# Row coefficients laid out by kind, sequence and token before GpSimd reads them across x by features

## The chip, the cores and the metric

One core of a Trainium2 chip runs the whole program. The metric is the device time in microseconds of one execution, from its start to its end.

## The reference, cut to what matters

The input x has 4 sequences of 4096 tokens of 512 features. A causal linear attention block and a linear layer with quantised operands follow each other, each between two layer norms and with a residual:

```python
x = x + layernorm(attn(layernorm(x)))          # linear attention, 16 heads of 32, elu(.)+1 feature map
x = x + layernorm(ffn(layernorm(x)))           # ffn: 512x512, both operands quantised in blocks of 32
# attn: q, k, v = x @ W.T + b; running sums over tokens of k v^T and of k;
#       out = (q . kv_cum) / max(q . k_cum, 1e-6);  then @ Wo.T + bo
```

The part that the change touches is the first layer norm. It has one scale and one shift for each token: `x * rstd(token) + shift(token)`.

## The kernel before, in words

The work is cut into 32 tiles. A tile is 128 tokens of each of the 4 sequences, so 512 rows of x. A loop of turns is written out by hand: turn i does the matmuls of q, k, v, scores, attention and output of tile i, the linear layer of tile i-1, and the norm of x for tile i+1. Each engine has its own list of instructions in a fixed order, and semaphores join the lists. TensorE (PE) does 240 matmuls of 128x512 in a turn and many small ones.

The norm of x is applied to x **by features**: the 128 partitions are features, and along the free axis lie 4 groups of features times 128 tokens. In that layout a token's coefficients vary along the free axis and are the same in each partition, so they have to be copied to all partitions. This goes over DRAM, in these steps:

- VectorE (DVE) takes the mean and variance of the 4 sequences of the tile, with tokens as partitions. GpSimd (POOL) makes from them `coef`, 128 partitions (tokens) x 2 kinds (scale, shift) x 4 sequences (`rstd`, L1388 and L1391).
- SyncE (SP) stores `coef` in `coef_dram` (`store_coef`, L331), waits until it has landed, and loads all its 1024 numbers into each of the 128 partitions of `x_coef` (`spread_coef`, L337).
- SP loads x by features into `exp_t`, a buffer with two places (`load_xt`, L327).
- GpSimd multiplies `exp_t` by the scales (L1412) and adds the shifts (L1414), for each of the 4 sequences (`x_scale`). ScalarE (ACT) and DVE then split the result into `xT_hi` and `xT_lo` (L676, L960), the operands of the next tile's matmuls.

In a turn GpSimd does `x_scale` of sequences 0 and 1 between the outputs of tile i-1 (`output`, L1442) and `x_scale` of 2 and 3 after the first residual (`residual`, L1419).

SP has one queue in a fixed order. Around the two steps it holds: store `coef`, spread it, store the output of sequence 1 of the tile before (L354), load a residual tile (L320), load two `exp_t` (L327), store `rinv`, the inverses of the attention's denominators, in DRAM (`store_rden`, L343), and spread them over `kc` (`spread_rden`, L349). What comes back is used by DVE to scale the attention of sequence 0 (`normalise`, L1024). From there two ways lead to PE: ACT casts it to `oT_hi` (L735), DVE makes `oT_lo` (L1036), and PE multiplies both with Wo; behind `oT_lo` on DVE stand the masks of the scores (L1029), for which PE's attention of sequence 1 waits (L550).

Of the kernel before, what the change touches and what calls it, by code (L numbers as in the profile page):

```python
# [5 lines left out]
F32 = mybir.dt.float32  # L6
# [6 lines left out]
P = 128  # L13
NSEQ, LEN, D = 4, 4096, 512
HEADS, DH = 16, 32
G = D // P
HPG = P // DH
TILES = LEN // P
ROWS = NSEQ * P
# [35 lines left out]
def count(tile, n, per=4):  # L55

    return tile * per + n + 1


def build(nc, x, xt, wq, wk, wv, wo, wf, bq, bk, bv, bo, bf, consts, out):  # L60
    ctx = ExitStack()
    with ctx:
        def sb(name, shape, dt=F32):
            return ctx.enter_context(nc.sbuf_tensor(name, shape, dt))
# [4 lines left out]
        def sem(name):  # L69
            return ctx.enter_context(nc.semaphore(name))  # L70
# [21 lines left out]
        x_in = sb("x_in", [P, NSEQ, D])  # L92


        x_coef = sb("x_coef", [P, P, 2, NSEQ])
        xT_hi = sb("xT_hi", [P, G, ROWS], F32R)
        xT_lo = sb("xT_lo", [P, G, ROWS], F32R)
        exp_t = sb("exp_t", [P, 2, ROWS])
# [36 lines left out]
        coef = sb("coef", [P, 2, NSEQ])  # L135
# [72 lines left out]
        coef_stored = sem("coef_stored")  # L208
# [52 lines left out]
        def by_group(flat):  # L261
            return flat.rearrange("p (g t) -> p g t", g=G)
# [25 lines left out]
        def kcq(ops, g):  # L288
            return ops.tensor_tensor(tokens(kc, g), tokens(kc, g), by_seq(QT[:, g, :]), ALU.mult)

        coef_dram = nc.dram_tensor("coef_dram", (P, 2, NSEQ), F32).ap()

        def x_cols(t, b):
            return t[:, :, b * P:(b + 1) * P]
# [9 lines left out]
        def _(sp):  # L304
# [23 lines left out]

            def store_coef(tile):
                sp.wait_ge(rstd_set["x"], count(tile, NSEQ - 1))  # L330
                sp.dma_start(coef_dram[:], coef[:]).then_inc(coef_stored, 16)  # L331

            def spread_coef(tile):
                sp.wait_ge(coef_stored, 16 * tile)
                if tile > 1:
                    sp.wait_ge(x_shifted, count(tile - 2, NSEQ - 1))
                sp.dma_start(x_coef[:].rearrange("p t k b -> p (t k b)"),  # L337
                             coef_dram.rearrange("t k b -> (t k b)").unsqueeze(0).to_broadcast([P, 2 * ROWS])
                             ).then_inc(coef_loaded, 16)

            def store_rden(tile):
# [14 lines left out]
            def turn(i, prev, cur, nxt):  # L356
# [9 lines left out]
                if nxt:  # L366
                    store_coef(i + 1)
                    spread_coef(i + 1)
# [1016 lines left out]
        def _(pool):  # L1385
# [16 lines left out]
            def turn(i, prev, cur, nxt):  # L1402
                def x_scale(tile, b):

                    def by_token(k):
                        return x_coef[:, :, k, b].unsqueeze(1).to_broadcast([P, G, P])

                    rows = by_group(exp_t[:, b % 2, :])
                    if b == 0:
                        pool.wait_ge(coef_loaded, 16 * tile)  # L1410
                    pool.wait_ge(xt_loaded[b], 16 * tile)
                    nc.gpsimd.tensor_tensor(rows, rows, by_token(0), ALU.mult).then_inc(x_scaled, 1)  # L1412
                    pool.wait_ge(x_scaled, count(tile - 1, b))
                    nc.gpsimd.tensor_tensor(rows, rows, by_token(1), ALU.add).then_inc(x_shifted, 1)  # L1414
# [179 lines left out]
```

## Time and profile before

| what | value |
|---|---|
| median of 3 runs | 2392.15 us (2386.2 to 2392.42) |
| the profiled execution, own time | 2392.45 us |
| its span in the profile | 2390.7 us |
| mean granted TensorE clock | 0.995 |
| PE busy | 2328.4 us (97%) |
| DVE busy | 1981.4 us (83%) |
| GpSimd busy | 1474.0 us (62%) |
| ACT busy | 1083.8 us (45%) |

The span is the stretch between the first and the last record of the execution; its own time is 1.75 us longer. The busy time of PE is modelled from its starts, so that a busy PE is not PE at its peak. An engine's idle time counts only where the engine that sets the end waits for it.

### The profile page before, as it was taken

To read this page: it belongs to the slowest core of one execution; us is meant where nothing else is said; L and a number is where in the kernel's file an instruction comes from. 1 tells how busy PE (TensorE), PEld (TensorE's weight loads), DVE (VectorE), ACT (ScalarE), POOL (GpSimd) and SP (SyncE) were. 2 spreads that over 40 slices of the span, in tenths; PEclk is the share of its full clock that TensorE was granted. 3 is DMA by queue.
4 is the path that set the end of the run, shared out by engine and by line. 5 is a ranking of instruction groups with operands and counts; after the bars stand their busy time and mean duration, and the time that the engine had idled before them with its cause. 6 is when DMAs were issued, how large, how long until landed. Compare 5 with 4: busy or idle time off the path is not lost.

```text
span 2390.7 us, 63829 instructions
## 1 busy us (share of the span) xinstructions
PE 2328.4 (97%) x26146; PEld 1902.4 (80%) x26146; DVE 1981.4 (83%) x3987; ACT 1083.8 (45%) x1840; POOL 1474.0 (62%) x1731
## 2 busy tenths in 40 slices
PE   7999999999999999999999999999999999999997
PEld 5878788888788788887888887888878888778885
DVE  7888788888788888888888887888888888878886
ACT  5444444444444444444444443444444444444442
POOL 4566666666566666666665665656666656656554
PEclk9999999999999999999999999999999999999999
DMA  5123222232222222222322222322123222222211
GB/s 170 60 91 100 73 83 68 75 99 87 80 71 71 91 100 73 82 67 77 99 78 90 71 69 91 99 73 82 63 82 100 73 91 73 71 91 95 77 46 36
DMA packets 108227, 195.55 MB, mean 82 GB/s; under 512 B 15136, under 2 KB 21664, under 8 KB 107424
## 3 DMA queue, kind: packets, MB, share of 16 engines
q1 hardware_dynamic: 107936, 191.47, 24.1%
q8 instruction: 206, 3.38, 0.6%
q14 instruction: 85, 0.70, 0.1%
HBM read 155.65 MB, written 35.78 MB: 80 GB/s over the span
## 4 chain that ended last, share of the span: by engine, by line
PE 77%; DMA 8%; ACT 4%; DVE 4%; issue 3%; POOL 2%; SPq 2%; POOLq 0%; DVEq 0%; ACTq 0%
PE work L428 11%; PE work L430 11%; PE work L429 11%; PE score L428 10%; PE score L429 10%; PE score L430 10%; PE work L550 4%; PE work L447 4%; DMA rden_dram<-rinv 4%; PE score L513 4%; DMA kc<-rden_dram 4%; PE state_bank L563 1%; POOL f_buf L1442 1%; ACT f_buf L680 1%; POOL rs_f L1388 1%
## 5 line engine op out<-in xcount | busy, mean ns | idle before, releaser
L1029 DVE TENSOR_TENSOR A<-score,causal 128x512 f32<-128x512 f32 x512 | 329.6, 682 | 21.3 <-PE score L513 21.1
L1412 POOL TENSOR_TENSOR exp_t<-exp_t,x_coef 128x512 f32<-128x512 f32 x124 | 198.3, 1599 | 141.4 <-DMA exp_t<-in_xt 141.4
L735 ACT CAST oT_hi<-kc 128x512 fp32r<-128x512 f32 x128 | 79.8, 624 | 365.0 <-DVE kc L1024 365.0
L1419 POOL TENSOR_TENSOR x_res<-x_res,o_buf 128x512 f32<-128x512 f32 x128 | 175.6, 1372 | 105.6 <-ACT o_buf L680 105.6
L428 PE MATMUL work<-wo_hi,oT_hi 128*128 128x512 f32 x512 | 204.6, 400 | 16.4 <-ACT Kn L730 13.6
L428 PE MATMUL work<-wv_hi,xT_hi 128*128 128x512 f32 x512 | 214.0, 418 | 0.7 <-issue 0.7
L1414 POOL TENSOR_TENSOR exp_t<-exp_t,x_coef 128x512 f32<-128x512 f32 x124 | 205.7, 1659 | 9.7
L428 PE MATMUL score<-xT_hi,wq_hi 128*128 128x512 f32 x512 | 206.8, 404 | 2.1 <-DVE KT L969 2.1
L428 PE MATMUL score<-xT_hi,wk_hi 128*128 128x512 f32 x512 | 205.9, 402 | 0.7 <-DVE xT_lo L960 0.7
L429 PE MATMUL work<-wv_lo,xT_hi 128*128 128x512 f32 x512 | 201.1, 393 | 0.8 <-issue 0.8
L430 PE MATMUL work<-wv_hi,xT_lo 128*128 128x512 f32 x512 | 201.8, 394 | 0.0
L429 PE MATMUL score<-xT_lo,wq_hi 128*128 128x512 f32 x512 | 200.8, 392 | 0.0
L430 PE MATMUL work<-wo_hi,oT_lo 128*128 128x512 f32 x512 | 200.4, 391 | 0.0
L429 PE MATMUL work<-wo_lo,oT_hi 128*128 128x512 f32 x512 | 200.3, 391 | 0.0
L430 PE MATMUL score<-xT_hi,wq_lo 128*128 128x512 f32 x512 | 200.3, 391 | 0.0
L429 PE MATMUL score<-xT_lo,wk_hi 128*128 128x512 f32 x512 | 199.8, 390 | 0.0
L430 PE MATMUL score<-xT_hi,wk_lo 128*128 128x512 f32 x512 | 199.6, 390 | 0.0
L1428 POOL TENSOR_TENSOR xd<-q,xs 128x512 f32<-128x512 fp8e4 x128 | 134.2, 1048 | 88.9 <-DVE q L1071 83.2
L1442 POOL TENSOR_TENSOR f_buf<-f_buf,x_res 128x512 f32<-128x512 f32 x96 | 136.2, 1418 | 85.6 <-ACT f_buf L680 85.6
L1388 POOL TENSOR_TENSOR rs_f<-ve_f,minus_half 128x1 f32<-128x1 f32 x128 | 81.8, 639 | 162.8 <-DVE ve_f L950 162.8
L680 ACT ACTIVATE o_buf<-x_res,shift_r,rs_r 128x512 f32<-128x512 f32 x128 | 104.5, 817 | 138.7 <-POOL shift_r L1391 138.7
L699 ACT ACTIVATE exp_t<-exp_t 128x512 f32<-128x512 f32 x256 | 162.5, 635 | 8.1
(134 smaller groups left out, 6394.9 us busy)
## 6 DMA issues: line engine op xcount, KB each, us to landing
x_in<-in_x SPq DMA_DIRECT2D x128, 256.0 KB, 4.5
kc<-rden_dram SPq DMA_DIRECT2D x128, 256.0 KB
x_res<-in_x SPq DMA_DIRECT2D x128, 256.0 KB, 2.8
exp_t<-in_xt SPq DMA_DIRECT2D x124, 256.0 KB, 3.0
out<-f_buf SPq DMA_DIRECT2D x96, 256.0 KB, 2.0
x_coef<-coef_dram SPq DMA_DIRECT2D x31, 512.0 KB, 3.6
out<-xd SPq DMA_DIRECT2D x32, 256.0 KB, 2.1
rden_dram<-rinv SPq DMA_DIRECT2D x32, 64.0 KB, 3.4
```

The costliest lines, as they stand in the source:

```text
L428: nc.tensor.matmul(dst, st_hi(c), mv_hi(c), start=(c == 0), stop=False)
L429: nc.tensor.matmul(dst, st_hi(c), mv_lo(c), start=False, stop=False)
L430: last = nc.tensor.matmul(dst, st_lo(c), mv_hi(c), start=False, stop=(c == G - 1))
L680: return nc.scalar.activation(dst, src, ACT.Identity, bias=shift[n][:, b:b + 1], scale=rs[n][:, b:b + 1])
L699: nc.scalar.activation(exp_t[:, g % 2, :], exp_t[:, g % 2, :], ACT.Exp, scale=-1.0).then_inc(exp_done, 1)
L1029: nc.vector.tensor_tensor(A[:, j, :, :], score_bank[j][:], causal[:].unsqueeze(1).to_broadcast([P, G, P]), ALU.mult).then_inc(a_set, 1)
L1388: nc.gpsimd.tensor_tensor(rs[n][:, b:b + 1], ve[n][:, b:b + 1], minus_half[:], ALU.pow).then_inc(rs_set[n], 1)
L1412: nc.gpsimd.tensor_tensor(rows, rows, by_token(0), ALU.mult).then_inc(x_scaled, 1)
L1414: nc.gpsimd.tensor_tensor(rows, rows, by_token(1), ALU.add).then_inc(x_shifted, 1)
L1419: nc.gpsimd.tensor_tensor(x_res[:, b, :], x_res[:, b, :], o_buf[:, b % 2, :], ALU.add).then_inc(r_set, 1)
L1428: nc.gpsimd.tensor_tensor(xd[:].rearrange("p (n k) -> p n k", k=BLOCK), q8[:, b, :].rearrange("p (n k) -> p n k", k=BLOCK), xs[:, b, :].un ...
L1442: nc.gpsimd.tensor_tensor(f_out[b], f_out[b], x_res[:, b, :], ALU.add).then_inc(out_set, 1)
```

## The change

The coefficients get another order in DRAM and in SBUF. Before, the 8 numbers of a token (2 kinds x 4 sequences) lay beside each other; now the 128 tokens of one kind and one sequence do. The store of `coef` writes 1024 single numbers, 8 from each partition, each 512 bytes from the next. The spread copies the same 4 KB to each partition as before. GpSimd's second operand in L1412 and L1414 had a step of 8 numbers (32 bytes) from token to token, and now has a step of 1.

```diff
-        x_coef = sb("x_coef", [P, P, 2, NSEQ])
+        x_coef = sb("x_coef", [P, 2, NSEQ, P])
...
-        coef_dram = nc.dram_tensor("coef_dram", (P, 2, NSEQ), F32).ap()
+        coef_dram = nc.dram_tensor("coef_dram", (2, NSEQ, P), F32).ap()
...
             def store_coef(tile):
                 sp.wait_ge(rstd_set["x"], count(tile, NSEQ - 1))
-                sp.dma_start(coef_dram[:], coef[:]).then_inc(coef_stored, 16)
+                sp.dma_start(coef_dram.rearrange("k b t -> t k b"), coef[:],
+                             allow_slow_non_contiguous=True).then_inc(coef_stored, 16)
...
-                sp.dma_start(x_coef[:].rearrange("p t k b -> p (t k b)"),
-                             coef_dram.rearrange("t k b -> (t k b)").unsqueeze(0).to_broadcast([P, 2 * ROWS])
+                sp.dma_start(x_coef[:].rearrange("p k b t -> p (k b t)"),
+                             coef_dram.rearrange("k b t -> (k b t)").unsqueeze(0).to_broadcast([P, 2 * ROWS])
...
                     def by_token(k):
-                        return x_coef[:, :, k, b].unsqueeze(1).to_broadcast([P, G, P])
+                        return x_coef[:, k, b, :].unsqueeze(1).to_broadcast([P, G, P])
```

No engine's list of instructions changes its order. The one instruction with another form in the list is the store on SP, which was 128x8 and is 128x8x1.

## Rows read from the trace of the kernel before

**Rows 1.** The page, part 1: busy us, share of the span, instructions.

```profile
PE 2328.4 (97%) x26146; PEld 1902.4 (80%) x26146; DVE 1981.4 (83%) x3987; ACT 1083.8 (45%) x1840; POOL 1474.0 (62%) x1731
```

**Rows 2.** Windows, 12 to 24 us after each coef store: length, PE busy; clock, DMA share, GB/s.

```profile
1008.95:1020.95 12.00, 12.00 (x228) 1.00 0.38 131
1080.87:1092.87 12.00, 10.09 (x193) 1.00 0.42 132
...
sum 372.00, PE 354.54; mean PE 11.44
...
sum 108.00, PE 102.97; mean PE 11.44
...
sum 108.00, PE 96.51; mean PE 10.72
```

**Rows 3.** The chain that ended last, in two turns: start us, us, what.

```profile
563.38 3.37 DMA rden_dram<-rinv
...
570.49 0.70 DVE kc L1024
...
571.87 2.15 DVE oT_lo L1036
...
577.73 1.08 PE work L550 x32
...
1075.92 4.84 DMA rden_dram<-rinv
```

**Rows 4.** DVE busy in L1036 alone, summed over nine stretches of 8.70 us.

```profile
sum 78.30, DVE 17.74; mean DVE 1.97
```

**Rows 5.** Timeline of GpSimd in the turn from 556.33 us.

```profile
565.89 1.65 POOL L1412 TENSOR_TENSOR exp_t<-exp_t,x_coef 128x512 f32<-128x512 f32 x1 [4.36 <-DMA exp_t<-in_xt]
...
570.14 1.56 POOL L1412 TENSOR_TENSOR exp_t<-exp_t,x_coef 128x512 f32<-128x512 f32 x1
571.78 1.69 POOL L1414 TENSOR_TENSOR exp_t<-exp_t,x_coef 128x512 f32<-128x512 f32 x1
```

**Rows 6.** Timeline of DVE and of GpSimd in the turn from 996.95 us.

```profile
1012.27 0.69 DVE L1036 TENSOR_TENSOR oT_lo<-kc,oT_hi 128x512 fp32r<-128x512 f32 x1 [0.69 <-ACT oT_hi L735]
...
1012.29 2.20 POOL L1414 TENSOR_TENSOR exp_t<-exp_t,x_coef 128x512 f32<-128x512 f32 x1
```

**Rows 7.** GpSimd's operations by tile: duration ns min/median/max, first and last start.

```profile
L1412 POOL TENSOR_TENSOR exp_t<-exp_t,x_coef x124: 1517/1611/1699, 53.9 to 2272.5; 128x512 f32<-128x512 f32 x124
L1414 POOL TENSOR_TENSOR exp_t<-exp_t,x_coef x124: 1518/1610/2229, 55.5 to 2274.2; 128x512 f32<-128x512 f32 x124
...
L1419 POOL TENSOR_TENSOR x_res<-x_res,o_buf x128: 1275/1298/1620, 70.5 to 2367.3; 128x512 f32<-128x512 f32 x128
...
L1442 POOL TENSOR_TENSOR f_buf<-f_buf,x_res x96: 1267/1290/1673, 110.2 to 2383.0; 128x512 f32<-128x512 f32 x96
```

**Rows 8.** Timeline of SP in the turn from 1216.18 us: start, us of issuing.

```profile
1216.18 0.33 SPq L331 DMA_DIRECT2D coef_dram<-coef  x1
1217.59 0.33 SPq L337 DMA_DIRECT2D x_coef<-coef_dram  x1
1221.40 0.34 SPq L354 DMA_DIRECT2D out<-f_buf  x1
...
1223.29 0.43 SPq L343 DMA_DIRECT2D rden_dram<-rinv  x1
```

**Rows 9.** Windows of the DMA engines: stretch, length, clock, share busy of 16, GB/s.

```profile
1216.18:1217.00 0.82, 1.00 0.00 0
1217.00:1217.20 0.20, 1.00 0.39 21
1217.20:1218.92 1.72, 1.00 0.02 5
1218.92:1220.66 1.74, 1.00 0.72 290
1220.66:1222.24 1.58, 1.00 0.07 23
...
1223.08:1225.48 2.40, 1.00 0.87 299
...
6.95:8.70 1.75, 1.00 1.11 328
```

**Rows 10.** SP's issues of the four weight loads at the start, min/median/max ns.

```profile
L398 SPq DMA_DIRECT2D V<-in_wk x4: 620/632/662, 3.2 to 5.3; - x4
```

## The prediction

> **What bounds the kernel now.** The page's part on busy time comes first. PE is busy in 97% of the span and GpSimd in 62% [rows 1], so 2390.7 less 2328.4, some 62 us, is all the idle time that PE has, with the start and the end of the program in it. A faster GpSimd is worth something only where PE waits, now, for what GpSimd holds up.
>
> So I looked for PE's idle time by its place in the turn. The 31 stores of the coefficients mark the turns. In the stretch from 12 to 24 us after each store PE is busy for 354.54 of 372 us, so it is idle for 17.5 us [rows 2]. I read the chain of waits and the timeline of this stretch in each turn, and the turns fall in three kinds. The second and the third sum in rows 2 are those of nine turns each:
>
> - In nine turns `oT_lo` of sequence 0 (L1036) takes 1.54 us or more, 1.97 us on average, where it takes 0.69 us elsewhere [rows 4, 6]. PE is idle for 108 less 102.97, 5.0 us, in these.
> - In nine others the store of `rinv` lands late, as the one that takes 4.84 us where another takes 3.37 [rows 3]. PE is idle for 11.5 us in these, 1.9 us in the one shown [rows 2].
> - In the other thirteen it is idle for 17.5 - 5.0 - 11.5 = 0.9 us in all; one of them has none [rows 2].
>
> The first kind is where GpSimd comes in. In the turn from 556.33 us the chain goes from the store of `rinv` over DVE's `normalise` to `oT_lo`, 2.15 us long, and on to the masks and PE's L550 [rows 3]. GpSimd began the addition of the shifts of sequence 1 at 571.78, 0.09 us before `oT_lo` at 571.87, and ended it at 573.47; `oT_lo` ended at 574.02, a little over 0.5 us after that [rows 3, 5]. In the turn from 996.95 us DVE was first by 0.02 us: `oT_lo` took its 0.69 and the addition took 2.20 us, where its median is 1.61 [rows 6, 7]. Of these two operations, whichever comes second does not run until the first is done. The Trainium skill says so too ("SBUF — State Buffer", on the shared port pair: an exclusive lock between a GpSimd operation and a DVE one with two SBUF inputs, held for the whole instruction); both have two inputs in SBUF, and the trace agrees.
>
> **The change part by part.**
>
> *GpSimd's 248 operations on `x_coef`.* Their medians are 1.61 us, their minima 1.52 [rows 7]. The nearest operations with the same shape, two inputs and the output in place, but no step, have medians of 1.298 and 1.290 us [rows 7]. I take 1.29 to 1.30: 0.31 us less for each, 248 x 0.31 = 77 us of GpSimd's busy time. The bounds are 1.27 (the least of those rows) and 1.61 (the step costs nothing, and something else made them longer). A row of the Trainium skill ("GPSIMD Engine Reference", Performance pitfalls) has a read with a step of over 8 bytes at 2.9 cycles for an element against 1.9. The trace shows less, 1.61 against 1.29, or 25%. By the page's ratio 1.61 would become 1.05, and the sum below would gain at most the last half microsecond of the nine turns.
>
> None of the 77 us lies on PE's path by itself. The first of the eight in a turn starts when its `exp_t` has landed, after 4.36 us of idle [rows 5].
>
> *The collision.* In the turn from 556.33 us three operations on `x_coef` lie between the landing of `exp_t` and the addition that collides. Each is 0.31 us shorter, so the addition starts at 571.78 - 0.93 = 570.85 and ends at 572.15. `oT_lo` is asked for at 571.87 and waits for 0.3 us and not 1.5. The block of 1.46 us cost PE about 5.0 / 9 = 0.56 us in a turn, so the masks have some 0.9 us to spare behind it, and 0.3 us costs nothing. The gain is the idle of the nine turns above what the thirteen have: 5.0 - 9 x 0.07 = 4.4 us. In the thirteen a block of about 0.3 us may be new, where DVE was first until now; it is within the same 0.9 us, and I count it as nothing. With that cover gone it would be 13 x 0.3 = 4 us. The nine late turns wait for a DMA, and I leave them as they are.
>
> *The store of `coef`.* Now 128 packets of 32 bytes. SP issues it at 1216.18, nothing moves for 0.82 us, the packets pass in 0.20 us with the DMA engines busy 0.39 of it, and SP goes on at 1217.59 [rows 8, 9]. So the 1.41 us are 0.82, 0.20 and 0.39 of receipt. The 0.20 us hold 8 packets for each of 16 engines, 25 ns for a packet. After the change there are 1024 packets of 4 bytes, 64 for each engine. 64 x 25 ns = 1.6 us, so it lands after 0.82 + 1.6 + 0.39 = 2.8 us. That this pace can be kept up over a long run is seen at the start: packets of 512 bytes pass at 328 GB/s over 1.75 us [rows 9], which is 1.56 ns for a packet or 25 ns on each engine. Four times as many packets of one DMA made SP's issue 0.63 us long [rows 10] against 0.33 [rows 8]. That 0.3 us may or may not come before the first packet.
>
> The bounds of the landing: below, 0.82 + 64 x (0.39 x 25 ns = 10 ns) + 0.39 = 1.85 us, when only the busy part of a packet counts. Above, all of the 1.41 us grows with the eightfold packets, 11.3 us. I take 2.8, since 0.82 and 0.39 are times without packets in the rows.
>
> *What is queued behind it.* On SP the spread of the coefficients, then the store of the output at 1221.40, which waits for GpSimd [rows 8]. SP is free from 1217.92 to 1221.40, so its own slack is 3.5 us. The DMA engines have less: they move the spread's 512 KB until 1220.66, have next to nothing until 1222.24, and are then busy with the output, the residual and two `exp_t` up to the packets of `rinv` [rows 9]. A spread that is up to 1.58 us late fills a hole; one that is later pushes `rinv` and the chain above by the rest. So the store may land up to 1.41 + 1.58 = 3.0 us after its issue. 2.8 is inside: 0 us. GpSimd itself does not feel 1.4 us: the spread's last packets pass 4.48 us after the store [rows 8, 9], and its first operation starts 565.89 - 556.33 = 9.56 us after it, when `exp_t` has landed [rows 5]. Beyond 3.0 us each microsecond costs what the late turns show: a landing 1.5 us later (4.84 against 3.37) [rows 3] made PE idle for 11.5 / 9 - 0.07 = 1.2 us, 0.8 us for each, so 31 x 0.8 = 25 us for each microsecond.
>
> **Sum.** 2392.45 (own time of the profiled execution, 0.3 above the median of the runs) - 4.4 + 0 = 2388.0 us. A measurement of this kernel can tell about 0.3%, 7.2 us, from no change: the three runs lie 6.2 us apart.
>
> **The rivals.**
>
> - *The store is too slow (slower).* Single numbers written 512 bytes apart cost more than 25 ns each. It decides from 3.0 us of landing, 28 ns for a packet, which is only 3 ns above my value. At 40 ns it lands at 3.8 us and the time is 2388 + 0.8 x 25 = 2408; at 60 ns at 5.05 us and 2439; at the upper bound of 11.3 us some 2595. For it: the margin is thin, and no row has packets of 4 bytes to DRAM. Against it: the packets of 32 bytes were busy for only 10 ns of their 25. The Trainium skill ("DMA: Bandwidth & Descriptors") advises against this form: a last dimension that is not contiguous is one descriptor per element, and under 512 bytes there is a read-modify-write. It names no price for one; no row before shows 4 bytes. Chance 0.25 that it costs over 7 us beyond the gain.
> - *The relief spreads (faster).* GpSimd is through with sequences 2 and 3 up to 8 x 0.31 = 2.5 us earlier in the turn, and other blocks of DVE go too. If all the idle of the nine and thirteen turns goes (5.9 us) and a fifth of the late turns' (2.3), the time is 2384. Against it: those late turns wait for a transfer. Chance 0.22 of a gain over 7 us.
> - *New collisions (about the same).* DVE is blocked a little in every turn and the block of 0.3 us does cost: 2388 + 4 = 2392. Chance 0.13. It is in the chance of no change.
> - *The step costs GpSimd nothing.* The operations stay at 1.61 us, the collisions stay, and the time is 2392. Chance 0.05, since 1.52 is the least of 248.
>
> **How the numbers follow.** The forecast has 0.35 and its own range is 2384 to 2392. The prediction is its value, 2388. Faster by over 0.3%, below 2385.3: 0.24, the second rival and the forecast's lower end. Slower by over 0.3%, above 2399.3: 0.27, the first rival. The rest, 0.49, within. The range leaves a tenth out below, 2381. Above it takes in a landing of up to about 4.1 us, 2388 + 1.1 x 25 = 2416.
>
> **What would show it.** GpSimd: L1412 and L1415 with medians near 1.30 us, its busy time near 1397 us. SP: the spread issued 2.8 us after the store, and the output's store still 5.22 us after it. DMA: the hole before the output's store down from 1.58 to about 0.2 us, and `rinv` landing after 3.4 us as before. DVE: no `oT_lo` of sequence 0 near 2 us, but many of 0.8 to 1.1. PE: idle in the stretch from 12 to 24 us near 13 us in place of 17.5. Wrong would be a spread issued over 3 us after the store, with the landing of `rinv` later by as much.

## The result and the profile after

The changed kernel takes 2607.15 us, the median of 6 runs (2603.47 to 2609.02), against 2392.28 us for the kernel before. The ratio is 1.0897, with an interval of 1.0881 to 1.0913: 9% slower, outside the range of the prediction and on the side of its first rival. The profiled execution took 2603.73 us, 211.3 more than that of before.

The busy times of the page, where rows 1 have 1474.0 us for POOL, and its groups of L1413 and of L538:

```profile
PE 2400.5 (92%) x26146; PEld 1951.5 (75%) x26146; DVE 1967.5 (76%) x3987; ACT 1085.1 (42%) x1840; POOL 1389.0 (53%) x1731
...
L1413 POOL TENSOR_TENSOR exp_t<-exp_t,x_coef 128x512 f32<-128x512 f32 x124 | 159.8, 1289 | 375.7 <-DMA exp_t<-in_xt 375.7
...
L538 PE MATMUL score<-QT,S 32*32 32x128 f32 x4096 | 86.6, 298 | 127.4 <-issue 127.0
```

GpSimd does what was forecast: 1289 ns for an operation on `x_coef` and 1389 us in all. PE, however, now stands still for 127 us ahead of L538, and the cause named is "issue": nothing that the profile shows had to be waited for. The store is where the two kernels part. SP's timeline in the turn from 1247.15 us (the counterpart of [rows 8]):

```profile
1247.15 0.38 SPq L331 DMA_DIRECT2D coef_dram<-coef  x1
1255.51 0.33 SPq L338 DMA_DIRECT2D x_coef<-coef_dram  x1
1255.88 0.43 SPq L355 DMA_DIRECT2D out<-f_buf  x1
1256.36 0.43 SPq L320 DMA_DIRECT2D x_res<-in_x  x1
1256.83 1.31 SPq L327 DMA_DIRECT2D exp_t<-in_xt  x2
1258.69 1.73 SPq L344 DMA_DIRECT2D rden_dram<-rinv  x1
1265.02 2.47 SPq L350 DMA_DIRECT2D kc<-rden_dram  x4
```

The spread follows 8.36 us after the store. Over the 31 turns it is 8.36 to 11.07 us with a median of 9.80; before it was 1.41, and 2.8 were forecast. The output's store follows 8.73 us after it, and stood at 5.22 in rows 8. The windows of the same turn show what the 8.36 us hold (length; PE, PEld, DVE, ACT, POOL busy; granted clock, DMA share, GB/s):

```profile
1247.15:1247.97 0.82, 0.82 (x6) 0.66 (x5) 0.73 (x2) 0.05 (x1) 0.00 (x0) 1.00 0.00 0
1247.97:1248.80 0.83, 0.83 (x7) 0.63 (x5) 0.83 (x4) 0.00 (x0) 0.07 (x1) 1.00 0.56 5
1248.80:1250.40 1.60, 1.60 (x102) 1.16 (x101) 1.60 (x4) 0.82 (x2) 1.12 (x2) 1.00 0.00 0
1250.40:1254.15 3.75, 0.02 (x2) 0.00 (x0) 0.65 (x2) 0.58 (x1) 1.26 (x1) 0.88 0.02 4
1254.15:1255.50 1.35, 1.35 (x37) 0.71 (x40) 0.00 (x0) 0.10 (x1) 0.00 (x0) 0.50 0.00 0
1255.50:1257.20 1.70, 1.70 (x29) 1.17 (x25) 0.00 (x0) 1.70 (x4) 0.00 (x0) 0.50 0.00 0
```

The 0.82 us without packets are there as before. The 1024 packets then pass within 0.83 us, at most 13 ns for each of an engine's 64, faster than my 25 ns. And then no data move for 6.7 us, until the receipt is there; the trace has only one packet of PE's instructions in that time. The time is not in the packets that the profile records but behind them. At 1250.4 PE stops for 3.73 us in the middle of a run of 128 equal matmuls, and after that the granted clock is 0.50, the lower of TensorE's two levels (1.2 GHz), where it had been 1.00. PE's timeline around the stop:

```profile
1248.90 1.52 PE L538 MATMUL score<-QT,S 32*32 32x128 f32 x100
...
1254.15 0.85 PE L538 MATMUL score<-QT,S 32*32 32x128 f32 x28 [3.73 <-issue]
```

All turns together, in windows of 0 to 12 us and of 12 to 24 us after the store, PE alone (the second answers to rows 2):

```profile
sum 372.00, PE 215.46; mean PE 6.95
...
sum 372.00, PE 367.07; mean PE 11.84
```

In the kernel before the first of these was 358.75 us. So PE's idle time in the first 12 us grew by 143.3 us; in the next 12 it fell from 17.5 to 4.9; in the third 12 us, where PE had none, it is 7.0. PE's busy time grew by 72.1 us with the same matmuls; the granted clock of the whole execution was 0.958 where it had been 0.995. That makes 143.3 - 12.6 + 7.0 + 72.1 = 210 of the 211 us. The waits confirm the place (us, times, longest); before, L537 and L501 waited for "issue" for 3.0 and 8.8 us in all:

```profile
POOL exp_t L1413 <- DMA exp_t<-in_xt: 375.7, 31, 15.9
...
DVE den L1010 <- PE work L502: 234.9, 32, 9.8
...
PE score L538 <- issue: 127.0, 36, 5.9
...
PE work L502 <- issue: 27.7, 7, 5.7
...
PE work L429 <- ACT Kn L731: 11.8, 8, 4.9
```

The last line is the wait in which a late `rinv` would reach PE. It was 13.6 us before and is 11.8 now: what PE loses in the changed kernel, it loses in the stops at L538 and L502 and at the lower clock after them.

### The profile page after: what moved, and what is told of

Read it like the earlier page. It is cut to its first block, busy times and chain, and to the rows that moved or that the text cites. A ratio compares the mean times of both kernels' runs of the same rounds, so it can differ in the third digit from the quotient of the medians.

```text
span 2601.9 us, 63829 instructions
## 1 busy us (share of the span) xinstructions
PE 2400.5 (92%) x26146; PEld 1951.5 (75%) x26146; DVE 1967.5 (76%) x3987; ACT 1085.1 (42%) x1840; POOL 1389.0 (53%) x1731
## 4 chain that ended last, share of the span: by engine, by line
PE 83%; issue 6%; DMA 5%; DVE 2%; ACT 1%; SPq 1%; POOL 0%; POOLq 0%; DVEq 0%; ACTq 0%
PE work L429 13%; PE work L430 12%; PE work L431 12%; PE score L429 9%; PE score L430 8%; PE score L431 8%; PE score L514 5%; PE work L551 5%; PE work L448 4%; PE score L538 3%; PE work L502 2%; DMA rden_dram<-rinv 2%; DMA coef_dram<-coef 2%; DMA kc<-rden_dram 1%; PE state_bank L564 1%
## 5 line engine op out<-in xcount | busy, mean ns | idle before, releaser
L1413 POOL TENSOR_TENSOR exp_t<-exp_t,x_coef 128x512 f32<-128x512 f32 x124 | 159.8, 1289 | 375.7 <-DMA exp_t<-in_xt 375.7
L429 PE MATMUL work<-wv_hi,xT_hi 128*128 128x512 f32 x512 | 227.7, 445 | 0.0
L429 PE MATMUL work<-wo_hi,oT_hi 128*128 128x512 f32 x512 | 202.0, 395 | 14.4 <-ACT Kn L731 11.8
L430 PE MATMUL work<-wv_lo,xT_hi 128*128 128x512 f32 x512 | 210.9, 412 | 0.0
L431 PE MATMUL work<-wv_hi,xT_lo 128*128 128x512 f32 x512 | 209.2, 409 | 0.0
L538 PE MATMUL score<-QT,S 32*32 32x128 f32 x4096 | 86.6, 298 | 127.4 <-issue 127.0
L1010 DVE TENSOR_SCALAR den<-work 128x128 f32<-128x128 f32 x32 | 9.3, 292 | 234.9 <-PE work L502 234.9
L538 PEld LDWEIGHTS score<-QT,S 32*32 32x32 f32 x4096 | 56.2, 107 | 150.3 <-issue 146.5
```

What stands on the lines that cost most here:

```text
L429: nc.tensor.matmul(dst, st_hi(c), mv_hi(c), start=(c == 0), stop=False)
L430: nc.tensor.matmul(dst, st_hi(c), mv_lo(c), start=False, stop=False)
L431: last = nc.tensor.matmul(dst, st_lo(c), mv_hi(c), start=False, stop=(c == G - 1))
L538: last = nc.tensor.matmul(score_bank[j][g * DH:(g + 1) * DH, b, :], S[rows, b, g, :], QT[rows, g, b * P:(b + 1) * P], start=True, stop=True)
```

## Two questions and two theories for each

**Why does the store land late?** Either 1024 packets of 4 bytes are too many, or it matters where in DRAM they go: single numbers side by side, written by different packets.

**Why does that cost 211 us?** Either because SP is held, so that everything behind the store and at last `rinv` is late (the way the prediction costed), or because writes that drain slowly stop other traffic, and PE with it, whether somebody waits for them or not.

A turn, from one store to the next, is the measure that needs the fewest words: 73.12 us before and 79.84 after; 6.72 x 31 = 208 us.

## The experiments on the cost

**e1_packed_read: the read alone.** The kernel before, with `x_coef` laid out as in the change and DRAM left as it was. The numbers so reach `exp_t` in the wrong places; the operations and their sizes are the same.

```diff
-        x_coef = sb("x_coef", [P, P, 2, NSEQ])
+        x_coef = sb("x_coef", [P, 2, NSEQ, P])
...
-                        return x_coef[:, :, k, b].unsqueeze(1).to_broadcast([P, G, P])
+                        return x_coef[:, k, b, :].unsqueeze(1).to_broadcast([P, G, P])
```

> The store of coef and its landing stay as before (128 packets of 32 bytes, 1.41 us); only GpSimd reads x_coef with a step of 1. The numbers in x_coef are not put in the new order, so x by features gets other coefficients: the time is read, not the values. If the terms of the prediction other than the store are right: L1412 and L1414 at 1.29 us, no oT_lo of sequence 0 near 2 us, PE idle 12 to 24 us after the store about 13 us in place of 17.5, and 2388 us. Rival: the blocks of DVE only move to other operations, 2392 us and no change.

Measured: 2380.2 us (2376.09 to 2382.01), ratio 0.996 [0.9946, 0.9975]. GpSimd's operations by tile, and PE's windows of 12 to 24 us after the store:

```profile
L1412 POOL TENSOR_TENSOR exp_t<-exp_t,x_coef x124: 1264/1288/1310, 52.7 to 2259.9; 128x512 f32<-128x512 f32 x124
```
```profile
sum 372.00, PE 363.14; mean PE 11.71
```

The half of the change that reads is a gain of 10 us, and the store is the whole loss. PE's idle time in the stretch is 8.9 us, where 17.5 were and 13 were forecast, so the gain is larger than 4.4. The longest `oT_lo` of sequence 0 is 1.19 us: none is near 2 us. The profiled execution is 12.2 us shorter than that of before. PE's idle time is 6.2 us of it: 8.6 less in this stretch, which is more than the nine blocked turns had, and some 2.5 more in the first 12 us. The other 6.0 us are busy time of PE with the same matmuls (2322.4 against 2328.4), which the prediction left out. Why it fell is not settled.

**e2_slow_store_unwaited: the same writes, and nobody waits for them.** The kernel before, its fast store and spread kept, and after the spread a store of the change's pattern into a tensor that nobody reads.

```diff
+            def dummy(tile):
...
+                sp.dma_start(dummy_dram.rearrange("k b t -> t k b"), ident[:, 0:8],
+                             allow_slow_non_contiguous=True).then_inc(dummy_stored, 16)
...
                     spread_coef(i + 1)
+                    dummy(i + 1)
```

> The kernel before, and behind the spread one more store of 1024 single numbers 512 bytes apart to a DRAM tensor of its own, for which only the next such store waits, a turn later. Theory A (instruction supply): while these writes drain, the transfers that bring PE its instructions do not get through, so PE stops in L537 or L501 in each turn although nothing waits for the store: 3 to 5 us idle there and some 2 us of lower clock, 2490 to 2600 us. Theory B (SP is held, and rinv is stored late): nothing holds SP here, so 2392 to 2400 us.

Measured: 2611.93 us (2607.85 to 2615.64), ratio 1.0932 [1.0913, 1.0951]: as large a loss as that of the changed kernel, and a little larger. SP's timeline in one turn, 1249.74 us being the store of `coef`:

```profile
1251.52 0.44 SPq L348 DMA_DIRECT2D dummy_dram<-ident  x1
1254.95 0.34 SPq L364 DMA_DIRECT2D out<-f_buf  x1
...
1256.78 0.43 SPq L353 DMA_DIRECT2D rden_dram<-rinv  x1
1266.64 2.46 SPq L359 DMA_DIRECT2D kc<-rden_dram  x4
```

The output's store is 5.21 us after the store of `coef`, as in the kernel before, and `rinv` goes out at 7.04. SP isn't held. But `rinv` needs 9.86 us to land here (median 9.2, before 3.4). The windows show why (columns as above):

```profile
1255.50:1258.00 2.50, 2.50 (x12) 1.93 (x11) 1.14 (x3) 0.59 (x1) 0.00 (x0) 1.00 1.17 97
...
1260.00:1262.00 2.00, 2.00 (x10) 1.64 (x9) 1.94 (x5) 0.59 (x1) 0.00 (x0) 1.00 0.89 41
```

The DMA engines are as busy as in rows 9 (0.87 at 299 GB/s), and move 97 and 41 GB/s: per byte they are busy four and seven times as long (1.17 / 97 and 0.89 / 41 against 0.87 / 299). In the first of these windows the trace has almost only packets of 2048 bytes, and the longest of them took 5.7 us, where the median is 0.09. Slow writes that drain slow down the transfers behind them.

**e3_slow_store_at_k: the same writes some 41 us later.** As e2, with the extra store behind the loads of x for the next tile, where PE does matmuls of 512 columns.

```diff
                     load_x(i + 1, 3)
+                    dummy(i + 1)
```

> The same unwaited store of 1024 single numbers, but issued behind the four loads of x_in, some 41 us after the coefficients' store, where PE does matmuls of 512 columns (0.23 us for each) and so uses few instructions in a microsecond. Theory A: PE has instructions for some 8 us at this pace, and the loss is under 1 us a turn, 2392 to 2425 us. Rival: writes that drain stop PE or its operands wherever they fall, and the loss is that of the run with the store behind the spread.

Measured: 2398.89 us (2395.37 to 2406.48), ratio 1.0039 [1.0021, 1.0057]. The store itself is as slow here, by its tile:

```profile
DMA to landing us min/median/max: 9.2/10.5/15.2
```

So the writes are not dear of themselves. The extra store costs 9 us where nothing urgent follows, and 222 where `exp_t` and `rinv` do.

**e7_slow_store_at_o: about 20 us after the store of `coef`**, ahead of the other two `exp_t`, again in the kernel before.

```diff
                 if nxt:
+                    dummy(i + 1)
                     load_xt(i + 1, 2)
                     load_xt(i + 1, 3)
```

> The kernel before, and the unwaited store in the change's pattern behind the load of the residual of sequence 2, some 20 us after the coefficients' store: PE does the attention, the states, the scores and the output there, 96 to 112 small matmuls between blocks of 24 large ones, and rinv has long landed. Theory A (PE's instructions do not come while the writes drain): PE stops between 22 and 36 us after the coefficients' store, with nothing in the profile that it waits for, and the loss is 1 to 5 us a turn, 2420 to 2550 us. Rival (only the transfers of SP behind the writes are late, here the loads of exp_t and the store of the output, which have slack): 2390 to 2400 us.

Measured: 2569.85 us (2560.09 to 2573.69), ratio 1.0737 [1.071, 1.0765]. That is above what either side had expected. The waits:

```profile
POOL exp_t L1423 <- DMA exp_t<-in_xt: 310.9, 61, 6.5
...
ACT xT_hi L687 <- POOL exp_t L1425: 214.0, 31, 9.8
...
PE work L439 <- DVE oT_lo L1047: 78.4, 52, 3.5
```

In the kernel before GpSimd waited for `exp_t` in 31 places and 141.4 us; here it is 61 places: the two loads behind the writes are late in each turn as well, and the next operands with them. PE's largest wait is now for `oT_lo`, 78.4 us in 52 places, where it was 2.5 in one. PE's waits for "issue" at L548 and L512 are 5.7 and 10.1 us, none over 2.6. So here late operands cost more than stops without a cause; the step from the late `exp_t` to the late `oT_lo` was not followed turn by turn.

**e4_hold_sp and e5_hold_sp_5: SP held, and no slow write.** The kernel before, with six (e4) or five (e5) more fast stores of `coef` ahead of the real one, each waited for.

```diff
+                for n in range(HOLD):
+                    sp.dma_start(hold_dram[:], coef[:]).then_inc(held, 16)
+                    sp.wait_ge(held, 16 * (HOLD * (tile - 1) + n + 1))
                 sp.dma_start(coef_dram[:], coef[:]).then_inc(coef_stored, 16)
```

> The kernel before, and ahead of the store of coef six more fast stores of the same 4 KB, each waited for (6 x 1.41 us), so that SP goes on 9.8 us after the first, as in the changed kernel, but with no slow write. Theory B: the output's store comes 5 us later, rinv is stored 5 us later, PE waits for the attention's scaling in the stretch from 16 to 24 us, 31 x 5 x 0.8 = 124 us more, 2516 us; and this alone would come near the changed kernel. Theory A says the same for this run by itself, but with no stop of PE in L537: the clock stays near 1.0 from 4 to 12 us after the store.

> As the run with six waited stores ahead of the store of coef, with five. It held SP 11.2 to 12.6 us there, where the changed kernel has a median of 9.8. One less should hold SP some 10 us, and rinv and the spread over kc come near 17.7 us after the first store, as in the changed kernel. If that lateness alone is worth the changed kernel's loss, turns of 80 to 82 us and 2600 to 2670 us; if the stop of PE in L537 is needed for it, well under 2600.

Measured: e4 2720.49 us (2720.09 to 2726.25), ratio 1.1395 [1.1373, 1.1416]; e5 2669.39 us (2664.87 to 2677.43), ratio 1.118 [1.116, 1.12]. For e4 2516 us were expected, with the price of the prediction. In e4 the spread came 11.9 us after the first store (the median), in e5 10.7, somewhat later than the changed kernel's 9.80. The waits of e5:

```profile
DVE kc L1030 <- DMA kc<-rden_dram: 283.5, 31, 10.5
...
PE work L434 <- ACT Kn L736: 236.6, 31, 9.1
```

This is the way of the prediction: `rinv` comes back late, `normalise` waits in each of 31 turns, ACT stands behind it, and PE waits for ACT's `Kn`. There is no long stop for "issue" in L543 (5.9 us in all, the longest 2.3). The first spread of `rinv` is issued 18.8 us after the first store instead of 11.17, and a turn lasts 81.91 us instead of 73.12: 8.79 / 7.6 = 1.15 us for each microsecond, where I had 0.8. In e4 it is (83.71 - 73.12) / (19.92 - 11.17) = 1.21. Part of it is the clock: 1.00 until PE stops, 0.50 behind the stop.

By that price the changed kernel, whose first spread of `rinv` is issued at 17.68, would lose 6.5 x 1.15 = 7.5 us in a turn. It loses 6.72, with other waits. So holding SP with fast stores is enough by itself for a loss of this size, but in the changed kernel PE hardly waits that way: 11.8 us for `Kn` where e5 has 236.6. SP is held about as long in both, so the stops at L538 and L502 come from the slow writes and not from the waiting. That the two losses don't add up, because PE doesn't miss while it stands what it would wait for later, is my reading. No run has PE's stops with `rinv` in time.

## The experiments on the store

**e8_numbers_apart: as many packets of the same size, elsewhere.** The changed kernel, whose stores from the second tile on put each of the 1024 numbers into 512 bytes of its own. The spread still reads `coef_dram`, so all tiles use the first tile's numbers.

```diff
-                sp.dma_start(coef_dram.rearrange("k b t -> t k b"), coef[:],
-                             allow_slow_non_contiguous=True).then_inc(coef_stored, 16)
...
+                    sp.dma_start(apart[:, :, 0:1], coef[:].rearrange("p k b -> p (k b)").unsqueeze(2),
+                                 allow_slow_non_contiguous=True).then_inc(coef_stored, 16)
```

> The changed kernel, but from the second tile on its store puts the same 1024 single numbers each into 512 bytes of their own, in another DRAM tensor; the spread goes on reading what the first tile stored, so all later tiles get the first tile's coefficients. As many packets of 4 bytes, the same waits. Theory L (numbers that share a piece of DRAM queue up): the store lands in 1.9 to 3 us and the time is 2380 to 2400 us. Theory N (single numbers to DRAM are slow wherever they go): 9 to 10 us and 2600 us.

Measured: 2379.93 us (2377.2 to 2381.27), ratio 0.9946 [0.9929, 0.9963]. The store's tile:

```profile
L336 SPq DMA_DIRECT2D apart<-coef x30: 554/560/605, 116.3 to 2230.3; - x30
...
DMA to landing us min/median/max: 2.6/2.8/4.1
```

This is the prediction's 2.8 us, and with it the gain is there and nothing is lost. The number of packets, their 4 bytes and the step in SBUF are those of the change. The addresses differ, and the spread reads a tensor that these stores don't write.

**m1_probe_stores, m2_probe_spacing, m3_probe_neighbours: which addresses.** The kernel before with one more store in each turn, of a kind that changes from turn to turn, at the place of e3. SP waits for it, and a marker behind it shows when it landed. In m1 the probe stands behind the loads of x and has 2 to 4 us of them in its time; in m2 and m3 a store that is waited for goes first, so that nothing is ahead of the probe.

```diff
+                sp.dma_start(marker_a[:], ident[:, 0:8]).then_inc(probed, 16)
+                sp.wait_ge(probed, 48 * tile - 32)
...
+                if kind == 1:
+                    sp.dma_start(near[0:P, 0:1], ident[:, 0:1], allow_slow_non_contiguous=True).then_inc(probed, 16)
...
+                if kind == 4:
+                    sp.dma_start(by32[:, 0:1], ident[:, 0:1], allow_slow_non_contiguous=True).then_inc(probed, 16)
```

> The kernel before, and behind the four loads of x_in in each turn, where SP has nothing to do for over 20 us, one extra store from the identity matrix, waited for, and then a marker store of 128 packets of 32 bytes, waited for too. The time from the extra store's issue to the marker's issue is its landing. Eight kinds take turns, four or three turns each: (0) 128 x 32 bytes side by side, as the coefficients before; (1) 128 x 4 bytes side by side; (2) 128 x 4 bytes, 4096 bytes apart; (3) 1024 x 4 bytes in the order of the change; (4) 1024 x 4 bytes, each in 512 bytes of its own; (5) the same with 32 bytes; (6) the same with 64 bytes; (7) 1024 x 4 bytes into SBUF. Kind 0: 1.4 us. Theory L (numbers that share a piece of DRAM queue up for it): (3) some 9.8 us and (1) well over 1.4 us for its size, (4) to (6) 3 us or less. Theory N (each small write to DRAM costs, wherever it goes): (3), (4) and (5) all near 8 to 10 us, (6) less or the same, (7) under 3 us. Theory G (it is the making of 1024 descriptors): (3) to (7) all near 8 to 10 us.

> As the run with eight kinds of extra store, but each one waits first for a marker, so that it starts with nothing ahead of it. Kinds: (0) 128 x 32 bytes side by side; 128 x 4 bytes with a distance of 4 (1), 8 (2), 16 (3), 32 (4) and 64 bytes (5); (6) 16 x 4 bytes side by side; (7) the change's 1024 x 4 bytes. Theory L with pieces of 64 bytes whose writes go one by one, at a price for each: (1) and (7) the same, 5 to 8 us, (2) half of what (1) has over 1.4, (3) a quarter, (4) an eighth, (5) 1.4 us, and (6) as (1), since its 16 numbers are one full piece. If the unit is larger, say 512 bytes, (6) is an eighth of (1) and (2) to (5) fall no faster than that unit says.

> As the run with the spacings. Kinds: (0) 128 x 4 bytes into the same 512 bytes as (1), but partition 8q + a goes to number 16a + q, so that the eight numbers of partitions 8q to 8q + 7 lie 64 bytes apart and each run of 16 neighbours comes from 16 groups of partitions; (1) 128 x 4 bytes in the order of the partitions; (2) the first 32 partitions only; (3) the first 64; (4) 256 x 4 bytes, two rows of 128; (5) the change's 1024. Theory E (a DMA engine has a group of 8 partitions, and its writes to neighbouring numbers go one behind the other): (0) 1.4 to 2 us although all 128 numbers are neighbours as in (1); (1) 7.0; (2) two for each engine and some 2.2 us, (3) four and some 3.8; (4) as (1). Theory M (the memory takes neighbouring numbers one by one, whoever sends them): (0) 7.0 as (1), (2) and (3) by the count, 2.7 and 4.2.

The whole kernels took 2391.64, 2395.78 and 2394.79 us, each one run. From the list of DMAs of m1 (KB, median us to landing); the 0.5 KB in `scratch_flat` are side by side and those in `scratch` 4096 bytes apart, the 4 KB in `scratch_kbt` are the change's pattern and those in `scratch` in part 1024 numbers 512 bytes apart:

```profile
scratch_flat<-ident SPq DMA_DIRECT2D x4, 0.5 KB, 8.5
scratch<-ident SPq DMA_DIRECT2D x4, 0.5 KB, 3.8
scratch_kbt<-ident SPq DMA_DIRECT2D x4, 4.0 KB, 9.5
in_sbuf<-ident SPq DMA_DIRECT2D x3, 4.0 KB, 5.0
```

128 numbers side by side are nearly as slow as 1024 in eight rows, and twice as slow as 128 apart. 1024 numbers 512 bytes apart took 4.3 to 5.4 us, and so did 1024 pieces of 32 or of 64 bytes (4.1 to 5.3). Into SBUF, 1024 numbers at 8 bytes' distance took 4.4 to 5.1.

In m2 and m3, from the issue of the probe to that of the marker behind it:

| what is stored | landed after, us |
|---|---|
| 128 pieces of 32 bytes, side by side | 1.42 |
| 128 numbers, 64 bytes from one to the next | 1.41 |
| the same at 32 bytes | 1.41 to 1.49 |
| at 16 bytes | 1.41 to 2.41 |
| at 8 bytes | 2.73 to 3.22 |
| at 4 bytes, side by side (m2, m3) | 6.84 to 7.41 |
| side by side, neighbours from partitions 8 apart | 5.91 to 7.81 |
| only 64, side by side | 6.27 to 7.29 |
| only 32 | 2.92 to 3.46 |
| only 16 | 1.33 |
| 2 rows of 128 | 7.28 to 9.14 |
| 8 rows of 128, the change's pattern | 8.36 to 10.66 |

Two of m3's probes in SP's timeline, first 32 numbers side by side, then the 128 of permuted partitions, each with its marker:

```profile
1921.16 0.33 SPq L358 DMA_DIRECT2D near<-ident  x1
1924.34 0.33 SPq L366 DMA_DIRECT2D marker_c<-ident  x1
...
2214.03 0.58 SPq L354 DMA_DIRECT2D near<-ident  x1
2221.84 0.33 SPq L366 DMA_DIRECT2D marker_c<-ident  x1
```

Two things follow. From 32 bytes of distance on, the distance costs nothing; below, the store gets slower as more numbers lie in the same 32 bytes. And it doesn't matter who sends: with the partitions permuted, so that other packets are neighbours, it is as slow. Theory E is out by that; the delay is then in the memory or on the way to it, and no run separates the two. How the numbers add up stays open. 16 side by side cost nothing, though eight of them share 32 bytes; theory L of m2 had put them as high as 128. 64 cost 5 to 6 us, where theory M had 4.2 us in all, and eight rows cost only 1 to 4 us more than one. So numbers close together are the cause, and writes that wait one by one for a piece of 32 bytes are not shown.

**e6_turned_on_dve: the change's layout with pieces of 128 bytes.** DVE transposes `coef`, padded to 32 columns, in 32x32 blocks into `coef_t`. In it 32 tokens of one kind and sequence lie side by side in a partition, and the store has 128 packets of 128 bytes. GpSimd reads as in the change.

```diff
+            def turn_coef(tile):
+                dve.wait_ge(rstd_set["x"], count(tile, NSEQ - 1))
+                nc.vector.transpose(coef_t[:], coef[:]).then_inc(coef_turned, 1)
...
-                sp.dma_start(coef_dram.rearrange("k b t -> t k b"), coef[:],
-                             allow_slow_non_contiguous=True).then_inc(coef_stored, 16)
+                sp.dma_start(coef_dram.rearrange("j q t -> q j t"), coef_t[:]).then_inc(coef_stored, 16)
```

> The changed kernel's order of the coefficients and GpSimd's reads with a step of 1, with a fast store: DVE transposes coef (128 x 32, padded) in blocks of 32 x 32 behind phi_q(3), and SP stores 128 pieces of 128 bytes. The store lands in 1.4 to 1.6 us, SP issues it about 1 us later in the turn, which the hole of 1.58 us in the DMA engines takes; DVE has 0.1 us more in a turn. If the packed read's gain (2380.2 us) is real and the store's landing was the whole loss: 2378 to 2388 us. If 1 us of lateness of the spread already pushes rinv: 2390 to 2410 us.

Measured: 2378.17 us (2376.0 to 2380.15), against 2387.86 before on the same chip, ratio 0.9956 [0.9943, 0.997]. SP's timeline in one turn:

```profile
1209.71 0.56 SPq L333 DMA_DIRECT2D coef_dram<-coef_t  x1
1211.68 0.33 SPq L339 DMA_DIRECT2D x_coef<-coef_dram  x1
1214.03 0.34 SPq L356 DMA_DIRECT2D out<-f_buf  x1
```

The store lands after 1.97 us, later than the 1.4 to 1.6 expected, and still within the slack. The kernel computes all of the reference. It is faster than both kernels of this case.

## Why the prediction was wrong, by its steps

- **GpSimd's operations, 1.61 to 1.29 or 1.30 us: right.** 1289 ns; 1389 us busy, with 1397 forecast. e1, e6 and e8 have the same.
- **The collision, -4.4 us: right mechanism, too small.** In e1 no `oT_lo` of sequence 0 is over 1.19 us. The gain is about 10 us there and in e6, and 12 in e8. The part beyond 4.4 us is mixed: idle time beyond that of the nine turns went in e1, so the late turns, which I had taken as fixed, gained too, and PE's busy time fell by 5 to 6 us in all three, for which the sum had no term. The cause of both stays open. (In the kernel before, `oT_lo` of sequence 0 took up to 0.91 us outside the nine turns, and not always the 0.69 that I wrote.)
- **The store, "64 x 25 ns = 1.6 us, so it lands after 2.8 us": the step that failed.** It measured 8.36 to 11.07 us, median 9.80. For packets that go to places of their own the total was right (e8: 2.8 us), and partly by luck: there the first packet comes after 1.2 us and not 0.82, the packets pass in 0.6 us in the median and not 1.6, and the receipt takes 0.9 and not 0.39. What the calculation left out is that the change puts numbers of different packets close together, eight in the same 32 bytes of DRAM. The row that I took the pace from has packets of 32 bytes; in m2 these are just large enough to cost nothing. The Trainium skill ("DMA: Bandwidth & Descriptors", Rules for kernel authors) advises against a last dimension that is not contiguous, and the changed kernel agrees: its store lands after 9.80 us and not 1.41. The runs show a finer picture: 1024 single numbers 512 bytes apart, the same form, cost 1.4 us more than 128 packets.
- **"0.82 and 0.39 are times without packets": wrong in the second half.** The receipt is not a fixed 0.39 us. It came 6.7 us after the last packet in the turn shown, and 0.9 us after it in e8. The upper bound, 11.3 us, with which everything grew eightfold, held; the reason that it gave, that every part grows with the packets, did not.
- **The slack up to 3.0 us: not contradicted.** With 2.8 us e8 lost nothing, and `rinv` took 3.6 us.
- **"Beyond 3.0 us each microsecond costs 25 us": wrong mechanism for this kernel.** For 9.8 us it would have given 2388 + 6.8 x 25 = 2558, and 2607 was measured. A late `rinv` alone costs 1.15 us in a turn for each microsecond and not 0.8 (e5); the granted clock falls behind its long stops, and rows with a delay of 1.5 us could not show that. And I costed only SP and what is queued on it. e2 holds nobody and loses 222 us: the writes that drain slow the transfers behind them, and PE stops. In the changed kernel the wait that the prediction priced is 11.8 us, and PE's stops without a cause are 155 us.
- **The first rival** named the right place and the point from which it decides, 3.0 us. It thought of a dearer packet (40 or 60 ns), and its price at 11.3 us, 2595, comes near the measured time in part because two errors partly cancel: a landing of 9.8 and not 11.3 us, and more than 25 us for each.

**PE's stop.** In the changed kernel and in e2 PE stops for 3 us and more within runs of matmuls, and the profile shows nothing that it waits for: 127.0 us in 36 waits at L538 and 27.7 in 7 at L502 in the changed kernel, and in e2 less, beside a wait for a late operand:

```profile
PE work L439 <- ACT Kn L741: 64.5, 17, 7.0
PE score L524 <- issue: 44.8, 9, 6.5
PE work L512 <- issue: 25.7, 7, 7.9
```

e3 and e5 have only what the kernel before has too. The page lists the DMA queue that brings PE's instructions:

```profile
q8 instruction: 206, 3.38, 0.6%
```

I had taken instructions that come late behind the slow writes as the reason. The traces can tell, and they say yes for e2 and no for the changed kernel. The 206 packets of q8 have 16384 bytes each, and PE has 52915 instructions, so a packet brings some 257 of them. If PE runs out of them, its stops should lie whole blocks apart in its list. In e2 PE has 18 stops of over 2 us that no semaphore ends, from the second tile on. The distances between them, counted in PE's instructions, are all multiples of 256: each is at position 193 of 256. PE goes on 5.5 to 9.2 us after the end of a packet of q8. The kernel before has three small stops of 2.2 to 2.4 us, also at position 193; they end 1.3 to 1.5 us after such a packet. In e2, then, PE's instructions come late behind the slow writes.

The changed kernel has 30 stops of 2.9 to 5.9 us, one in each turn from the second tile on. One of them is at position 193; the others are spread over the 256, so they are in the middle of blocks. They have a place in the turn instead: 19 of the 24 at L538 come when 199 to 207 of its 256 matmuls and weight loads are done. What PE lacks there stays open. e5 shows that it isn't SP's waiting, and e8 that it isn't the number of the packets. Every execution on record has a profile, so that a part that the recording itself plays can't be ruled out either.

## What to carry to other kernels

- A layout that makes a read cheaper is paid for by a write. In these runs packets that each had 32 bytes of DRAM to themselves cost nothing extra, and denser ones did. If the numbers lie across partitions, turn them on an engine first; the 32x32 transpose of one DVE instruction was enough here.
- The cost of a DMA is the time to its receipt and not that of its packets. Ask also what is queued behind it: the same slow store cost 9 us at one place of the turn, 178 at another and 222 at a third.
- A wait that is short in the trace gives a price for short waits. After the long ones here TensorE's lower clock came on top.
- A stop without a visible cause can have more than one. Where in its list of instructions the engine stands tells a late block of instructions (e2) from something else (the changed kernel).

## What the runs showed of the hardware

- 4-byte writes side by side in DRAM land slowly, whoever sends them: 128 in 6.8 to 7.4 us at 4 bytes of distance, about 3 at 8, 1.4 at 32 and more. Only 16 of them cost nothing (1.33 us).
- While such writes drain, other transfers keep the DMA engines busy (share 1.17) and move little (97 GB/s), and a store of 64 KB lands after 9.2 us and not after 3.4, though nothing waits for the slow one (e2). PE's instructions come late too: its 18 stops there, up to 7.9 us, are all at the same position of 256.
- The step of 32 bytes in GpSimd's second operand cost 25%: 1.61 against 1.29 us.
- TensorE's granted clock, 1.00 up to PE's stop, was 0.50 behind it, the lower level (1.2 GHz). Over the whole execution it was 0.958 where it had been 0.995, and PE's busy time grew by 72 us with the same matmuls.
